# Attention of the first head group: the row maxima spread over eleven pairs of steps, with six of them between the opening scores

## The reference

```
q, k, v = heads(ln(x) @ Wq.T), heads(ln(x) @ Wk.T), heads(ln(x) @ Wv.T)   # 16 heads of 32
q, k = rope(q), rope(k)
scores = where(causal, q @ k^T / sqrt(32), -inf)
x = x + merge(softmax(scores) @ v) @ Wo.T
x = x + ffn(ln(x))                       # base product + gated top-2 LoRA experts
```

## Time and profile before

| | us |
|---|---|
| median of 3 runs | 1549.22 |
| lowest, highest | 1548.52, 1552.3 |
| profiled execution, its own time | 1550.66 |
| span of the profiled execution | 1548.9 |
| PE busy | 1523.7 |
| DVE busy | 1132.8 |

### The profile page before, as it was taken

The page is one execution under the profiler, slowest core; times in us unless marked ns, Lnnn a source line. Parts: engine busy times, 40 slices in busy tenths (PEclk is TensorE's granted clock), DMA queues, the critical chain, the costliest instruction groups (busy, mean ns, idle before and its releaser), DMA issues.

```text
span 1548.9 us, 24844 instructions
## 1 busy us (share of the span) xinstructions
PE 1523.7 (98%) x9088; PEld 989.2 (64%) x9088; DVE 1132.8 (73%) x2269; ACT 756.4 (49%) x1540; POOL 890.5 (57%) x597
## 2 busy tenths in 40 slices
PE   7999999999999999999999999999999999999999
PEld 5888887755555555555555555555555547777777
DVE  6765656878877777777777878777777677666655
ACT  3222222135656656666666656665665673232221
POOL 2233332446878788888888797887797721121111
PEclk9999999979999999999999999999999999999999
DMA  5655685782476377468368359358445363223311
GB/s 204 211 190 204 207 266 185 225 187 61 90 167 148 83 160 162 89 140 182 84 137 191 83 127 202 83 116 197 100 99 134 88 147 109 82 82 105 134 61 55
DMA packets 120403, 215.83 MB, mean 139 GB/s; under 512 B 12504, under 2 KB 45784, under 8 KB 113112
## 3 DMA queue, kind: packets, MB, share of 16 engines
q1 hardware_dynamic: 102384, 136.20, 32.6%
q0 software_dynamic: 8064, 58.72, 18.4%
q10 hardware_dynamic: 9840, 19.40, 3.5%
HBM read 96.23 MB, written 58.72 MB: 100 GB/s over the span
## 4 chain that ended last, share of the span: by engine, by line
PE 92%; DVE 4%; DMA 2%; issue 1%; SPq 1%; ACT 1%; POOL 0%; POOLq 0%; DVEq 0%; ACTq 0%
PE a_mx L260 16%; PE a_st L1014 16%; PE a_av L1027 16%; PE p_pair L518 11%; PE f_wo_ps L1370 6%; PE p_v L530 5%; PE f_out_ps L1430 5%; PE a_sum L260 3%; PE a_sum L1049 2%; PE a_sum L1057 2%; DVE a_part L275 2%; PE f_out_ps L1445 1%; PE f_mid_ps L1370 1%; PE f_lg_ps L1400 1%; DMA a_gather<-a_pair 1%; PE a_mx L264 1%
## 5 line engine op out<-in xcount | busy, mean ns | idle before, releaser
L1114 ACT ACTIVATE a_probs<-a_st 128x512 f32<-128x512 f32 (+2 forms) x1244 | 573.6, 547 | 355.9 <-PE a_st L1014 347.2
L275 DVE TENSOR_REDUCE a_part<-a_mx 128x1 f32<-128x512 f32 (+2 forms) x773 | 495.4, 680 | 91.7 <-PE a_mx L260 78.9
L963 POOL TENSOR_TENSOR a_pair<-a_probs 128x1024 f32<-128x1024 f32 (+2 forms) x224 | 401.8, 1835 | 31.7 <-issue 16.4
L963 POOL TENSOR_TENSOR a_gather<-a_probs 128x1024 f32<-128x1024 f32 x76 | 179.9, 2388 | 84.5 <-ACT a_probs L1114 84.5
L392 POOL TENSOR_TENSOR p_rot<-p_mul 128x1024 f32<-128x1024 f32 x32 | 87.5, 2736 | 193.7 <-DVE p_mul L696 193.7
L1363 POOL TENSOR_TENSOR f_x<-f_x,f_bias 128x512 f32<-128x512 f32 x32 | 40.1, 1287 | 204.9 <-DVE f_xn L1580 204.9
L1027 PE MATMUL a_av<-a_probs,a_v 128*32 128x512 f32 (+3 forms) x1280 | 141.0, 540 | 2.2 <-POOL a_probs L944 2.2
L1027 PE MATMUL a_av<-a_probs,shared 128*32 128x512 f32 (+3 forms) x1280 | 142.6, 545 | 0.0
L278 DVE CUSTOM_DVE_ANT_0 a_mx<-a_mx,f_ctx 128x512 f32<-128x512 f32 (+1 forms) x155 | 94.7, 630 | 51.5 <-PE a_mx L260 51.5
L944 POOL TENSOR_SCALAR_AFFINE_SELECT a_probs<-a_probs 128x512 f32<-128x512 f32 x128 | 88.4, 755 | 64.2 <-ACT a_probs L1114 62.3
L1014 PE MATMUL a_st<-a_q_stack,a_k_stack 98*128 98x512 f32 (+3 forms) x287 | 101.8, 372 | 1.1 <-DMA a_q_stack<-a_neg_rows 1.1
(11 more groups left out here) (238 smaller groups left out, 3062.7 us busy)
## 6 DMA issues: line engine op xcount, KB each, us to landing
a_gather<-a_pair POOLq DMA_DIRECT2D x56, 1024.0 KB, 7.2
qk_scratch<-p_rot_hi SPq DMA_DIRECT2D x32, 512.0 KB, 3.1
qk_scratch<-p_rot_lo SPq DMA_DIRECT2D x32, 512.0 KB, 3.9
a_k_stack<-qk_scratch SPq DMA_DIRECT2D x60, 256.0 KB, 8.1
a_q_first<-qk_scratch SPq DMA_DIRECT2D x48, 256.0 KB, 7.0
a_third<-qk_scratch SPq DMA_DIRECT2D x36, 256.0 KB, 5.4
v_scratch<-p_v_st SPq DMA_DIRECT2D x32, 256.0 KB, 7.4
ctx_scratch<-a_ctx_st SPq DMA_DIRECT2D x32, 256.0 KB, 3.5
```

Source lines behind the costliest of these rows:

```text
L275: dve.tensor_reduce(found, scores.rearrange("p (h n) -> p h n", n=width), AX.X, ALU.max).then_inc(self.max_done, 1)
L963: pool.tensor_tensor(place[:, h:h + 2, q0:TT], probs[:, s % RING, h:h + 2, q0:TT], probs[:, (s + 1) % RING, h:h + 2, q0:TT], ALU.add).then ...
L1114: act.activation(probs[:, s % RING, h, q0:TT], score_bank(g, HG * s + h)[:, q0:TT], ACT.Exp, scale=SCORE_SCALE).then_inc(exp_done, 1)
```

## The change

Group 0 no longer takes 15 items a pair. Six of them (38 to 43) are put between the eight opening scores, those of pair 0 that stand ahead of the loop, one behind each of the first six. From there `items_before` draws a straight line to the pair before the last of each unit: unit 2's items end with pair 3 (before: in pair 2), unit 3's with pair 9, as before. The items of pairs 0 to 11 of group 0, from the counts of `items_before`:

| | opening | pairs 0 to 5 | pairs 6 to 11 |
|---|---|---|---|
| before | 0 | 15, 15, 15, 15, 8, 7 | 6, 8, 7, 7, 8, 8 |
| after | 6 | 9, 9, 9, 10, 9, 10 | 10, 10, 10, 10, 9, 8 |

Up to pair 5 these are 75 and 62 items, in pairs 6 to 11 44 and 57. From pair 12 on nothing differs but some bank numbers.

```diff
-PER_FIRST = 15
+UNIT_READY = [LAST_PAIR[t] - 1 for t in range(QT - 1)]
+OPENING = 6
+
 def items_before(p, first):
     steady = PLAN[p % NPAIR] + NITEM * (p // NPAIR)
-    return min(BEFORE_FIRST + PER_FIRST * p, steady) if first else steady
+    if not first:
+        return steady
+    since, have = 0, BEFORE_FIRST + OPENING
+    for t in range(2, QT):
+        due, need = UNIT_READY[t - 1], ITEM_END[t] + 1
+        if p <= due:
+            return min(steady, have + (need - have) * (p - since) // (due - since))
+        since, have = due, need
+    return steady
...
     banks, behind, ahead_of_sums, last_use = {}, {}, {}, [None] * MAX_BANKS
+    for item in range(BEFORE_FIRST, BEFORE_FIRST + OPENING):
+        bank = item % MAX_BANKS
+        banks[item], behind[item], last_use[bank] = bank, last_use[bank], item
...
             pe.wait_ge(first.mul_done, 4 * TILES + PROJECT_AHEAD)
-            for s in range(2):
-                for h in range(HG):
-                    scores(0, 0, s, h)
+            for n in range(2 * HG):
+                scores(0, 0, n // HG, n % HG)
+                if n < OPENING:
+                    item(0, 0, None, BEFORE_FIRST + n)
...
+            for k in range(BEFORE_FIRST, BEFORE_FIRST + OPENING):
+                first.item_max(dve, max_banks[BANK_OF_ITEM[k]], 0, k, dve_passed)
             group(0, True, False)
```

## The result

Over 22 executions of each kernel in turn on one chip, the changed one has a median of 1553.22 us (1549.18 to 1556.55) and the kernel before 1550.34 (1545.98 to 1554.61): a ratio of 1.0018, with a 95% interval of 1.0010 to 1.0026. That is 3 us slower, where the forecast said 6 us faster and the range ended at 1549. It is less than the 0.3% taken as the mark, but its interval is clear of 1.

The account below looks back on a forecast made before the run. PE was taken as the bound. Rows landing at 352.0, plus 7.0 (pair 5), 40.1 (pairs 6 to 11) and 1.7 (clock), put pair 11's end at 400.8, 6.2 us less: 1543.0 us, range 1537 to 1549.

Parts of the forecast that it names:

- The opening: Six items between the first eight scores: DVE starts 3.3 us earlier, and no fall of the clock at 313.
- The place of the stall: PE waits at pair 5's first score for unit 2's shift rows, from 345.7 to 352.0 us.
- the rows' landing, 352.0: Unit 2's shift rows, issued behind SP's loads, land and release PE at pair 5 at 352.0 us.
- both ends: Early and late limits for the shift rows' landing at pair 5: 347.5 and 353.8 us.
- The rule of turns by packets: DMA engines switch queues after each packet, so the rows pass within the gathering DMA, at 347.5; the forecast did not follow it.
- the clock, 1.7 us: After the wait at pair 5, one fall of the clock, 3.3 us at half, costing 1.7 us.
- the second rival: After the wait at pair 5 the clock stays low 13.6 us, costing 6.8 us: 1548.1 us; chance 0.12.
- pairs 6 to 11, 40.1 us: Group 0's pairs 6 to 11: 37.0 us before plus 3.1 us of PE for 13 more items.
- the third rival: DVE becomes the bound in pairs 6 to 11, which take 44.4 us: 1547.3 us; chance 0.1.
- It doesn't matter by how much I am wrong on pairs 0 to 4: Errors in pairs 0 to 4 don't change the sum as long as PE is at pair 5 before the shift rows.
- the first fall: In the kernel before, half clock from 313.0 to 326.7 us, 13.6 us, costing up to 6.8 us.

Follow-up runs that it names:

- e2: The changed kernel with the gathering DMA of group 0's pair 3 cut from 1 MB to 8 KB; 1549.54 us, ratio 0.9995 to the kernel before.
- e4: The changed kernel without the six opening items, the even spread and the wait kept; 1552.39 us, ratio 1.0017 to the kernel before.
- e1: The changed kernel with SP's 14 key and value loads for group 1 issued behind unit 2's shift rows; 1540.11 us, ratio 0.9934 to the kernel before.
- e5: The changed kernel with unit 2's four shift rows issued from ACT's queue, not SP's; 1547.60 us, ratio 0.9983 to the kernel before.
- e8: The changed kernel with 40 thrown-away score products that keep PE busy in the wait for the shift rows; 1551.30 us, ratio 1.0010 to the kernel before.
- e11: The same kernel as e8 (changed kernel, wait filled with 40 thrown-away score products), run again; 1550.08 us, ratio 1.0010 to the kernel before.
- e10: e1 without the six opening items, so the even spread with the loads behind the rows; 1543.45 us, ratio 0.9958 to the kernel before.
- e6: The kernel before with only the loads for group 1 moved behind unit 2's shift rows; 1549.17 us, ratio 0.9995 to the kernel before.

## Why the prediction was wrong

**What held.** The opening: item 38 stood 0.31 us behind the first score, 310.51 in place of 312.83, DVE's idle time ahead of it was 0.61 us in place of 3.81, and the clock was 1.00. PE reached pair 5 at 347.04, 36.8 us behind the first score, where 345.4 meant 35.9. The gathering DMA came at 335.58 (said: 334 to 336), SP's last load ended at 348.65 (said: 348.2). The place of the stall, its cause (SP's loads ahead of the rows, lengthened by the gathering DMA) and what is queued behind it were as put. From pair 12 on little changed: pair 11 ended 2.85 us later than before, the span 3.0.

**The term that failed first: the rows' landing, 352.0.** It was made of SP's last load at 348.2, an issue of 3.8 and a landing of 1.8 us, and then drawn from 353.8 to 352.0 towards the early end. The load was near, 348.65, and the issue took less, 2.6. The landing took 4.8 us. The 1.8 came from the last group, where SP's queue held no loads; here 0.37 MB in 2 us still stood on q1 ahead of the rows. e2 shows nearly the same landing without the gathering DMA (4.3), e4 a longer one (6.0), e1 a landing early enough not to be seen. The wait ended at 356.05, 4.05 us late, and outside of both ends; 0.7 of these arose ahead of `attend`, whose first score came at 310.20 in place of 309.51. The rule of turns by packets of the Trainium skill (DMA: Bandwidth & Descriptors, section on queues, rings and completion order), by which the forecast would have had it at 347.5, did not decide it. In 342 to 344 us q0 and q1 moved 48 and 59 packets as the profile counts them, which fits turns, but q1's 59 were 0.03 MB; in the 2 us ahead it was 32 beside 346, behind 39 beside 366. In e5's 345 to 348, q10 moved 8 beside 865 of q1, which is not turn by turn if q10's were ready by then, which no row shows.

**The second: the clock, 1.7 us.** One fall of 3.3 us was expected, like the second of before. It lasted 17.1 us, 11.3 of them on a busy PE, which is 5.6 us by half of it; pair 5 took 12.1 us where 7.0 + 1.7 was said, 3.4 us over. This is the mechanism of the second rival (13.6 us at half), on top of the forecast's own stall. e8 shows that the idle PE in the wait is what brings the fall: with the wait filled there was none. Of its price the medians show 2.5 us, the profiles 4.6 to 4.9.

**The third: pairs 6 to 11, 40.1 us.** They took 41.8 in every kernel with the spread, whatever stood ahead. The 13 more items were priced at 0.24 us, from one item that PE had followed at once. PE's busy time rose by 41.20 - 36.83 = 4.4 us, 0.34 an item, and the stretch by 4.7. In the timeline of PE the 44 items of before take 12.3 us from start to next start, 0.28 each, since the masked ones need two kinds of products, and the 57 of after 17.5, 0.31 each. So 13 at the mean of before would have been 3.6 us, only half a microsecond more than was said. Most of the rest lies where an item has no score to fill the time: pairs 6 to 9 have ten items and eight scores, so the last two items stand together, and these eight took 3.4 us, 0.43 each. In pair 6 (PE, then DVE):

```profile
372.85 0.99 PE L275 MATMUL a_mx<-a_k_first,a_q_stack 96*128 96x512 f32 x2
373.78 1.92 PE L1042 MATMUL a_av<-a_probs,shared 128*32 128x512 f32 x16
```
```profile
371.43 1.87 DVE L290 TENSOR_REDUCE a_part<-a_mx 128x1 f32<-128x512 f32 x3
373.22 0.67 DVE L290 TENSOR_REDUCE a_part<-a_sum 128x1 f32<-128x512 f32 x1
373.82 1.87 DVE L290 TENSOR_REDUCE a_part<-a_mx 128x2 f32<-128x512 f32 x3
```

DVE has no gap from 370.24 to 375.69, so I read the 0.93 us that PE spends on the two items as DVE's pace, not PE's; it shows as busy time of PE. Over the whole stretch DVE was busy 37.3 us (said: 37.7) of 41.8, so it was not the bound throughout, and the third rival's 44.4 did not come, but a piece of its mechanism did. (The share it was worked out from, 20.72 of 25, is 0.83 and not 0.85, which gives 45.5.)

The sum, in us late: 4.05 for the rows (0.7 of them from ahead of `attend`), 3.4 for pair 5 and its clock, 1.7 for pairs 6 to 11, 9.2 in all. 6.2 us less became 3.0 us more in the span, and 2.9 in the median.

**A step that held on paper only.** "It doesn't matter by how much I am wrong on pairs 0 to 4" is right, as e4 shows, but its other side was missed: whatever the opening won was thrown away, for the medians are the same with and without the opening items (1.0020 and 1.0017). Against before, unit 2's first score came at 356.05 in place of 364.08, 8.0 us won; from there to the end of pair 5 took 12.1 in place of 5.9, 6.2 lost; and the later items in pairs 6 to 11 cost 4.7.

**A comparison of profiles.** The kernel before does not lose the 6.8 us of the first fall in each execution. Over the 93 executions of it that were timed beside e1 to e11 its mean clock was between 0.991 and 0.999, and the time goes with it: a median of 1551.2 us in the 16 at 0.993, as in the profiled one, and 1545.8 in the seven at 0.999. So part of the gain that was counted on isn't there in a median: by the profiles e1 wins 11.7 us from start to end, by its ratio 10.2.

What stays open: how much of the gap between the clock's price by the profiles, 4.6 to 4.9 us, and by the medians, 2.5, is left once fast profiled executions are allowed for; what makes the landing take 4.3 to 6.0 us; and why e10 has no fall near 313 where before, e4 and e6, with the same opening, have one. The nine profiled executions with the opening items have none there.

## What to carry to other kernels

When a change makes a consumer arrive earlier, look at the queue of its last input, not only at when that input is ready: here four DMAs of 4 KB stood behind 17 loads whose first user, an item of group 1, came at 395.03 us, 39 us after the wait had ended, and moving 14 of the loads behind them turned 0.2% slower into 0.7% faster. Take the landing time of a small transfer from a place where its queue is as full as it will be. Price moved work by the mean of its kind, and see whether it will have other work between it there or stand together. Look at the spread of the clock over several executions before a fall of it in one profile is counted as a gain.

## What the runs showed of the hardware that was not expected

- Four DMAs of 4 KB behind queued loads on the same queue landed 4.8 us after their issue had ended (4.3 in e2, 6.0 in e4), against 1.8 us on a queue without loads.
- On a queue of its own (e5, q10) such rows did not overtake: 8 packets in 3 us beside 865 of q1, then 128 in the next 3 us.
- After 8.5 us in which PE did nothing the granted clock stayed at half for 11.3 us of busy PE; after 4.2 us (e2) for 12.3 us (351.55 to 363.8); after 3.1 us (e5) for 8.7 us (345.33 to 354.0); after 2.3 us (e4) there was no fall.
- In the 10 us over which q0 moved the 1 MB of the gathering DMA (338 to 348 us), q1 moved 1.12 MB; with 8 KB in its place (e2) it moved 1.73.
- The same opening of eight scores was at full clock in one kernel's profiled execution (e10) and at half in others: before for 13.6 us, e6 and e4 for 6.8 us (313.1 to 319.9 and 312.4 to 319.2).
